# One-hots of the last layer on ScalarE: an absolute difference and a relu, six pairs ahead

## The reference

```
p1   = tanh(p @ pp_W + pp_b)                         # per node
pair = concat(p1[src], p1[dst])                      # per edge, 128 wide
h    = ((pair @ pi_W1 + pi_b1) @ pi_W2).reshape(-1, 64, 8)
i1   = einsum('ecb,eb->ec', h, edge_attr_8)          # 8 basis values per edge
out  = p.at[src].add(tanh(i1 @ ii_W + ii_b))         # sum into the source node
```

## Time and profile before

| | us |
|---|---|
| median of three runs | 5185.09 (5183.49 to 5191.42) |
| the profiled execution | 5186.89 |
| its span, first to last instruction | 5185.1 |
| first multiply by the basis (L1151) in the last layer | 3917.05 |
| the seventh multiply from the end | 5136.15 |

### The profile page before, as it was taken

How to read it: one execution, slowest core, us unless ns; L and a number is a source line. 1 busy time by engine, 2 the same in 40 slices (tenths; PEclk the granted TensorE clock), 3 DMA queues, 4 the chain that set the end, 5 groups by cost and what they waited for, 6 DMA issues and landing times.

```text
span 5185.1 us, 117815 instructions
## 1 busy us (share of the span) xinstructions
PE 4338.7 (84%) x41609; PEld 3404.3 (66%) x41610; DVE 3795.9 (73%) x5814; ACT 1745.8 (34%) x3004; POOL 2008.5 (39%) x1717
## 2 busy tenths in 40 slices
PE   6999998888886977788489999579667888888886
PEld 3998888888885545344389999565444555555554
DVE  6988887877774028788466666456317999999998
ACT  0000000000000435788338777326222333333332
POOL 2888888885002017600000000000007666666663
PEclk6999999999997779999789999879668999999998
DMA  1000000000000000000000000000002111111113
GB/s 52 6 6 5 5 5 5 6 5 2 0 0 2 0 10 7 8 5 3 23 1 4 4 4 4 16 2 6 8 11 44 37 36 36 36 36 36 36 36 25
DMA packets 204304, 74.84 MB, mean 14 GB/s; under 512 B 169391, under 2 KB 189694, under 8 KB 204030
## 3 DMA queue, kind: packets, MB, share of 16 engines
q1 hardware_dynamic: 151710, 41.23, 3.6%
q0 software_dynamic: 52448, 31.60, 3.6%
HBM read 57.79 MB, written 14.88 MB: 14 GB/s over the span
## 4 chain that ended last, share of the span: by engine, by line
PE 52%; DVE 24%; issue 11%; POOL 3%; ACT 3%; DVEq 3%; DMA 2%; SPq 0%; ACTq 0%; POOLq 0%
PE ps L1201 51%; DVE adj L1159 8%; DVE scratch L861 5%; DVE adj L1151 4%; POOL by_src L512 3%; ACT scratch L651 2%; DVEq L859 1%; DVE adj L1164 1%; DVEq L338 1%; DVE scratch L1074 1%; DVE hwork L1049 0%; DMA r_dram<-adj 0%; DMA hwork<-gat_out_b 0%; DMA hwork<-gat_out_a 0%; DVE hwork L859 0%
## 5 line engine op out<-in xcount | busy, mean ns | idle before, releaser
L1201 PE MATMUL ps<-hwork,scratch 128*125 128x125 bf16 (+1 forms) x25750 | 1927.6, 236 | 102.6 <-DVE scratch L861 93.3
L1201 PEld LDWEIGHTS ps<-hwork,scratch 128*125 128x125 bf16 (+1 forms) x25750 | 1851.9, 151 | 172.1 <-DVE scratch L861 127.4
L512 POOL DMA_INDIRECT by_src<-work x782 | 1121.6, 1434 | 262.4 <-issue 224.3
L1074 DVE SCALAR_TENSOR_TENSOR scratch<-scratch,cols,adj 125x625 f32<-125x625 f32 x1125 | 939.9, 870 | 307.6 <-ACT scratch L651 289.8
L651 ACT ACTIVATE scratch<-work,cols 125x625 f32<-125x625 f32 x1125 | 965.0, 903 | 244.1 <-PE ps L1201 231.7
L541 POOL DMA_INDIRECT adj<-r_dram,adj x832 | 808.5, 972 | 493.9 <-DMA adj<-by_src 253.0
L861 DVE TENSOR_SCALAR scratch<-hwork,edge_ids 128x3125 bf16<-128x3125 uint16 x830 | 885.7, 1067 | 0.0
L1201 PEld LDWEIGHTS ps<-adj 128*125 128x125 f16 (+3 forms) x4320 | 386.4, 158 | 419.7 <-issue 381.5
L1201 PE MATMUL ps<-scratch,X 125*64 125x250 f32 (+3 forms) x3000 | 557.5, 458 | 113.2 <-DVE scratch L1074 99.8
L527 POOL IOTA adj<- 128x125 uint16 x1 | 0.2, 246 | 1635.1 <-DVEq L1123 1635.1
L1201 PE MATMUL ps<-work,adj 64*128 64x512 f32 x1664 | 470.6, 635 | 166.4 <-DVE adj L1151 122.1
(11 more groups left out here) (257 smaller groups left out, 2819.8 us busy)
## 6 DMA issues: line engine op xcount, KB each, us to landing
adj<-r_dram,adj POOLq DMA_INDIRECT x832
adj<-q_dram SPq DMA_DIRECT2D x416, 31.2 KB
by_src<-work POOLq DMA_INDIRECT x782
by_src<-adj SPq DMA_DIRECT2D x1, 4165.0 KB
adj<-by_src SPq DMA_DIRECT2D x104, 40.0 KB, 2.0
work<-in_rec SPq DMA_DIRECT2D x46, 85.0 KB, 1.9
gat_out_a<-hwork SPq DMA_DIRECT2D x5, 312.5 KB
hwork<-gat_out_a SPq DMA_DIRECT2D x1, 1562.5 KB
```

The costliest lines, as they stand in the source:

```text
L512: g.indirect_dma_start(by_src, bass.IndirectOffsetOnAxis(ap=pos_now[:, h, k:k + 1], axis=0), rec_in[:, h, k, :], None).then_inc(rec_sent[h ...
L1074: v.scalar_tensor_tensor(slots[:, j % SLOTS, :], slots[:, j % SLOTS, :], cols[:, 2, j, h:h + 1], adj3[:, j, ds(b * BW, BW)], ALU.add, ALU. ...
L1201: return t_.matmul(o_, l, r, start=start, stop=stop, skip_group_check=skip)
```

## The change

ACT builds the one-hots, for one pair at a time. For a column n and an edge with the relative source r it computes |r - n| (two activations per pair, one for each chunk, with `rel` as bias for each partition and a scale of -1) into the place of the one-hot, and then relu(1 - |r - n|) in place, one activation for both chunks. This happens in each step behind the hidden copy and ahead of `messages`, for the pair six ahead; six are built before the loop. `rel` becomes a 32-bit float and is made by DVE once per group (`relative`), ten to thirteen pairs ahead instead of six to nine; three groups are made before the loop. A semaphore `off_ready` orders the relu behind the differences. PE waits for the one-hots of every pair.

```diff
-        rel = at(o, CH, RING * GRP).bitcast(U16).rearrange(...)
+        rel = at(o, CH, 2 * RING * GRP).rearrange(...)
...
+            def onehots(i, n, k):
+                act.wait_ge(s["rel_ready"], RING * i + k // GRP + 1)
+                act.wait_ge(s["added"], M3_AHEAD + n + 1 - STEPS)
+                for c in range(2):
+                    last = a.activation(oh3[:, k, c, :], iota3, ACT.Abs, bias=rel[:, k // GRP, k % GRP, c:c + 1], scale=-1.0)
+                last.then_inc(s["off_ready"], 1)
+                act.wait_ge(s["off_ready"], n + 1)
+                a.activation(oh3[:, k], oh3[:, k], ACT.Relu, bias=ones[:, 0:1], scale=-1.0).then_inc(s["oh_ready"], 1)
...
                     turned_onehot(n, k)
                     if k > 0 or first_done(i):
                         hidden(n - 1, k + STEPS - 1)
+                    if k < STEPS - 6 or last_left(i):
+                        onehots(i if k < STEPS - 6 else i + 1, n + 6, (k + 6) % STEPS)
                     if k % 2 and (k >= 5 or first_done(i)):
                         messages(STEPS // 2 * i + (k - 5) // 2, (k - 5) // 2 + STEPS // 2)
+            act.wait_ge(s["consts"], 1)
+            for n in range(6):
+                onehots(0, n, n)
             turns(act_steps)(act)
...
-            def onehots(i, r, half):
-                a0 = GRP // 2 * half
+            def relative(i, r):
                 first = STEPS * i + GRP * r
-                if half == 0:
-                    dve.wait_ge(rec3_loaded[r], 16 * i + 16)
-                    v.tensor_tensor(rel[:, r], ..., ALU.subtract).then_inc(s["rel_ready"], 1)
-                dve.wait_ge(s["rel_ready"], RING * i + r + 1)
-                dve.wait_ge(s["added"], M3_AHEAD + first + a0 + 2 - STEPS)
-                v.tensor_tensor(oh3[:, GRP * r + a0:GRP * r + a0 + 2], ..., ALU.is_equal).then_inc(s["oh_ready"], 1)
+                dve.wait_ge(rec3_loaded[r], 16 * i + 16)
+                v.tensor_tensor(rel[:, r], ..., ALU.subtract).then_inc(s["rel_ready"], 1)
...
-            for r in range(2):
-                for half in range(2):
-                    onehots(0, r, half)
+            for r in range(3):
+                relative(0, r)
...
-                    if k % 4 >= 2 and (k < 8 or last_left(i)):
-                        onehots(i if k < 8 else i + 1, (k // GRP + 2) % RING, k % 2)
+                    if k % 4 == 2 and (k < 4 or last_left(i)):
+                        relative(i if k < 4 else i + 1, (k // GRP + 3) % RING)
...
-                if k % 2 == 0:
-                    pe.wait_ge(s["oh_ready"], STEPS // 2 * i + k // 2 + 1)
+                pe.wait_ge(s["oh_ready"], n + 1)
```

More of the change, by code:

```diff
@@ L201, in build_gnn @@
         base_now = at(o, CH, PAIRS).bitcast(I32); o += PAIRS
-        rel = at(o, CH, RING * GRP).bitcast(U16).rearrange("p (r a c) -> p r a c", r=RING, a=GRP); o += RING * GRP
+        rel = at(o, CH, 2 * RING * GRP).rearrange("p (r a c) -> p r a c", r=RING, a=GRP); o += 2 * RING * GRP
         iota3 = at(o, CH, 63).bitcast(U16)[:, 0:T]; o += 63
@@ L275, in build_gnn @@
             "ld", "w2T_ps", "w2T_ready", "wc_ps", "wc_ready", "ft_ps", "ft_ready", "p1_ps", "p1_ready", "qr_ps", "qr_ready",
-            "stored", "consts", "bias_ready", "rel_ready", "oh_ready", "ohT_ps", "ohT_ready", "hT_ps", "hT_ready", "g_ps",
+            "stored", "consts", "bias_ready", "rel_ready", "off_ready", "oh_ready", "ohT_ps", "ohT_ready", "hT_ps", "hT_ready", "g_ps",
             "prod_ready", "u_ready", "v_ready", "hi_ready", "lo_ready", "added", "sum_done", "out_stored", "pe_turn")}
@@ L1130, in _ @@
             dve.wait_ge(s["bias_ready"], 1)
-            dve.wait_ge(s["consts"], 1)
-            def onehots(i, r, half):
-                a0 = GRP // 2 * half
+            def relative(i, r):
                 first = STEPS * i + GRP * r
-                if half == 0:
-                    dve.wait_ge(rec3_loaded[r], 16 * i + 16)
-                    v.tensor_tensor(rel[:, r], rec[:, r, :, :, 0], base_now[:, ds(first, GRP)].unsqueeze(2).to_broadcast([CH, GRP, 2]),
-                                    ALU.subtract).then_inc(s["rel_ready"], 1)
-                dve.wait_ge(s["rel_ready"], RING * i + r + 1)
-                dve.wait_ge(s["added"], M3_AHEAD + first + a0 + 2 - STEPS)
-                v.tensor_tensor(oh3[:, GRP * r + a0:GRP * r + a0 + 2], iota3.unsqueeze(1).unsqueeze(1).to_broadcast([CH, 2, 2, T]),
-                                rel[:, r, a0:a0 + 2].unsqueeze(3).to_broadcast([CH, 2, 2, T]), ALU.is_equal).then_inc(s["oh_ready"], 1)
+                dve.wait_ge(rec3_loaded[r], 16 * i + 16)
+                v.tensor_tensor(rel[:, r], rec[:, r, :, :, 0], base_now[:, ds(first, GRP)].unsqueeze(2).to_broadcast([CH, GRP, 2]),
+                                ALU.subtract).then_inc(s["rel_ready"], 1)
             def products(n, k):
```

## The result

The changed kernel takes 5060.80 us (median of three, 5060.61 to 5067.19) against 5185.09 before: a ratio of 0.9761, 95% interval [0.9739, 0.9783], or 124 us less; 5065 was predicted, with a range of 5050 to 5095. The profiled execution took 5060.80 us (span 5059.0), 126.1 less than that of before. From the first multiply by the basis to the last, which I call the loop here, it took 1113.62 us against 1235.04 (3917.05 to 5152.09): 121.4 less, where the sum had 122. Of the other 4.7 us, 3.2 lie ahead of the last layer, where nothing was changed, and 1.5 in the loop's start: from the first relative sources to the first multiply 16.85 us passed against 18.31.

The account below looks back on a forecast made before the run. DVE, 98% busy in the last layer's loop, was taken as the bound. 1.19 us less in each of 102 cycles made 122 us, with other parts costed at nothing: 5186.9 - 122 = 5065 us, range 5050 to 5095.

Parts of the forecast that it names:

- DVE sets the pace: In the last layer's loop, DVE works 98% of 1219.1 us, nearly without a gap, and so bounds it.
- the plain step: A loop step on DVE with only the multiply and the sum that every step has; 2.58 us.
- Steps (1) to (4): DVE's cycle of four steps falls from 11.92 to 10.73 us, 1.19 won in each of 102 cycles, 122 us.
- the 2.98 step: The step of DVE's old cycle with a one-hot; without it 2.58, so 0.40 us won, not 0.59.
- The floor of 2.58: No step falls below 2.58 us: parts and multiply take turns on one pair of PSUM banks (the handshake).
- PE's own row of work is as long: PE's matmuls of the plain step, by themselves, also take the whole 2.58 us.
- Step (5): ACT's one-hot takes 1.25 us per pair, its work 4.70 of 5.36 per two pairs; copies stay covered, cost nothing.
- The rule: The Trainium skill's advice: relu and additions belong on VectorE; by it, a loss of 1.8 us engine time per two pairs.
- Steps (6) to (8): PE's wait for each pair's one-hots, the earlier relative sources and six one-hots before the loop (7.5 us) cost nothing.
- A: ACT's copies come late, PE waits 0.5 us in every other step; 104 us of gain go, about 5169; chance 0.12.
- B: ACT reloads its function table, 270 us slower, about 5455; decides from 1.27 us extra ACT time per two pairs; chance 0.04.
- C: Nothing is won, 5185 us, because what is behind DVE is as long as DVE; chance 0.04.

Follow-up runs that it names:

- e6: The kernel before, without the one-hot in every fourth step after the first turn; 5150.98 us, ratio 0.9937, loop 1199.20 us.
- e8: The changed kernel with the multiply by the basis done for one chunk of two after the first turn; 4999.07 us, ratio 0.9646, loop 1050.44 us.
- e1: The changed kernel with ACT's one-hots built only for the first 16 pairs and used again later; 5063.30 us, ratio 0.9758, loop 1111.58 us.
- e2: The changed kernel with one more ACT activation of 250 columns per pair; 5062.69 us, ratio 0.9758, loop 1113.52 us.
- e3: The changed kernel with two more ACT activations of 250 columns per pair; 5090.67 us, ratio 0.9812, loop 1140.37 us.
- e5: The changed kernel with each pair's turning done twice on PE, two more matmuls; 5060.46 us, ratio 0.9761, loop 1113.80 us.
- e10: The changed kernel with each pair's turning done four times on PE, six more matmuls; 5123.70 us, ratio 0.9885, loop 1178.03 us.
- e9: The changed kernel with half the multiply after the first turn and PE's low-half sums left out, two matmuls less; 5009.20 us, ratio 0.9661, loop 1059.02 us.

## Why the prediction was right

- **DVE sets the pace, 98% busy.** Right: what was taken from DVE came back as time, up to the floor of the plain step.
- **Steps (1) to (4), the cycle.** Right to 0.02 us in each step. The relative sources (L1139 before, L1151 now) cost 0.07 to the next start (0.10 taken); a one-hot in the 2.98 step is worth 0.40, which e6 shows by itself.
- **The floor of 2.58.** Right in size, wrong in one of its two reasons. The handshake holds it; "PE's own row of work is as long" was false by 0.09. The step that failed was to read a row without an idle gap as a row without slack: the same work takes 2.49 when the banks are free early (e8). The rows held a sign of it: inside the step each group of matmuls begins 0.08 or 0.16 ahead of the end of the one before it, and only the next `parts` begins 0.02 behind the earlier trace rows; in e8 it begins 0.07 ahead (4505.59). The error changed no term of the sum, as the handshake alone gives the floor.
- **Step (5), ACT.** The cover was right (e1, e2), the occupancy mis-sized: 4.70 us for two steps predicted, 3.91 measured (from e3), mostly as I added durations where starts count. The error lay on the safe side and changed no term of the sum. The price here is higher, 1.23 us on ACT for one pair against 0.34 on DVE, 3.6 times, with two passes over the columns (difference, relu) where DVE compared once; step (5) had 2.5 against 0.68, 3.7 times, and should not have called that agreement. The rule fails here all the same: 1.23 us on an engine with idle time costs at most 2 us of 1113 in all, and 0.34 on the one that sets the pace cost 121.
- **Steps (6) to (8).** PE's extra wait shows nowhere: with everything else as it is, its waits for DVE are the 0.16 to 0.29 of the late steps, and e1, which also drops the wait for the one-hots, gains 2.0 us at most. POOL waits 28.0 us of 400 for records (67.5 before), so it still had room. The six one-hots before the loop end at 3904, the first multiply is at 3912.35.
- **Rivals.** A is out by e1 and e2. B is out: no load in the loop. Its point of decision was rightly put on ACT's time for two steps, but at 1.27 us more it was too low: e3 adds 1.58, and its loop is still 95 us shorter than before. From the 3.91 it would be 5.97 - 3.91 = 2.06, an estimate that no run here tests. C is out, though its bounds exist, at 2.49.

## What to carry to other kernels

Moving work to an idle engine is worth the step it leaves, down to the next limit of that step, not the busy time it removes; read that limit from a step of the same loop that lacks the work. Count an engine's load from start to start in a stretch where it never waits, and not by adding durations. Once the floor of a step is known, spread what is late in some steps over those that have room.

## What the runs showed that was not expected

- PE showed no idle time between groups in a plain step of 2.58 and still took in two more matmuls (e5, +0.2 us in 1113.6); its row is 2.49 (e8, e10).
- Three limits lie within 0.1 us of each other: the handshake at 2.58, PE's row at 2.49, POOL's gathers at 9.94 / 4 = 2.49 from the rows of before, 9.99 / 4 = 2.50 in e8. In e9 the shorter row of PE gained nothing, and the loop was 8.6 us longer than in e8, as eight gathers took 10.12 us.
